# Self-attention scores from the 32 rows of each head, without the spread tile of keys

## The reference

```python
def _L1_attn_ref(x, W_qkv, b_qkv):            # H = 16 heads of D = 32
    b, t, _ = x.shape
    qkv = x @ W_qkv.T + b_qkv
    qkv = qkv.reshape(b, t, 3, H, D)
    q, k, v = (qkv[:, :, 0], qkv[:, :, 1], qkv[:, :, 2])
    q = _rope(q)
    k = _rope(k)
    q, k, v = (a.transpose(0, 2, 1, 3) for a in (q, k, v))
    scores = jnp.einsum('bhqd,bhkd->bhqk', q, k) / math.sqrt(D)
    w = jax.nn.softmax(scores, axis=-1)
    out = jnp.einsum('bhqk,bhkd->bhqd', w, v)
    return out.transpose(0, 2, 1, 3).reshape(b, t, E)
```

## Time and profile before

| | us |
|---|---|
| median of 3 runs | 2239.01 |
| the three runs | 2239.91, 2229.99, 2239.01 |
| the profiled execution | 2236.96 |
| its span (first to last instruction) | 2235.2 |
| projection block and its layer norm, from about 1972 to 2046.9 | 75 |
| attention block, from 2046.9 to 2085.1 | 38 |

### The profile page before, as it was taken

How to read it: one execution, slowest core, us unless ns; L and a number is a source line. 1 busy time by engine, 2 the same in 40 slices (tenths; PEclk the granted TensorE clock), 3 DMA queues, 4 the chain that set the end, 5 groups by cost and what they waited for, 6 DMA issues and landing times. The chain is left out here.

```text
span 2235.2 us, 44143 instructions
## 1 busy us (share of the span) xinstructions
PE 1971.9 (88%) x17800; PEld 1086.3 (49%) x17800; DVE 1626.0 (73%) x2842; ACT 994.2 (44%) x1404; POOL 680.1 (30%) x704
## 2 busy tenths in 40 slices
PE   6799999999597366999999999999999999767896
PEld 3355555555344223455555555555555555434542
DVE  4689999999565773587777777777777776446676
ACT  2689899989310332233333333333333333202332
POOL 3344444444210450133333333233333332121010
PEclk9899999999698577999999999999999999888898
DMA  4332333232131301000000000000000000110400
GB/s 142 96 80 73 87 95 89 69 82 58 31 136 52 127 1 58 21 22 19 4 22 22 21 22 22 21 22 22 21 22 22 21 2 2 48 71 0 156 0 19
DMA packets 40090, 106.16 MB, mean 47 GB/s; under 512 B 19280, under 2 KB 21584, under 8 KB 33744
## 3 DMA queue, kind: packets, MB, share of 16 engines
q1 hardware_dynamic: 39888, 103.35, 15.1%
HBM read 75.42 MB, written 1.05 MB: 34 GB/s over the span
## 5 line engine op out<-in xcount | busy, mean ns | idle before, releaser
L1360 POOL TENSOR_SCALAR a1c_p_hi<-a1c_pf 128x512 f16<-128x512 f32 x272 | 202.5, 745 | 663.8 <-ACT a1c_pf L1416 620.2
L365 POOL TENSOR_SCALAR a0c_p_hi<-a0c_r 128x1024 f16<-128x1024 f32 x128 | 154.9, 1210 | 268.9 <-DVE a0c_r L465 266.0
L1385 ACT ACTIVATE a1c_k_hi<-PS 128x512 f16<-128x512 f32 x136 | 81.2, 597 | 326.8 <-PE PS L1222 326.8
L470 DVE TENSOR_TENSOR a0c_p_lo<-a0c_r,a0c_p_hi 128x1024 f16<-128x1024 f32 x128 | 201.5, 1574 | 0.9 <-POOL a0c_p_hi L365 0.9
L1565 DVE TENSOR_TENSOR a1c_p_lo<-a1c_pf,a1c_p_hi 128x512 f16<-128x512 f32 x272 | 197.9, 729 | 5.5 <-POOL a1c_p_hi L1360 5.5
L1392 ACT ACTIVATE a1c_v_hi<-PS 128x512 f16<-128x512 f32 x136 | 81.6, 600 | 258.8 <-PE PS L1232 206.0
L1416 ACT ACTIVATE a1c_pf<-PS,a_maskc 128x512 f32<-128x512 f32 x256 | 175.1, 685 | 47.7 <-PE PS L1727 40.1
L1508 DVE CUSTOM_DVE_ANT_0 a1c_junk<-PS,a1c_maskr 128x512 bf16<-128x512 f32 x256 | 175.7, 686 | 18.4
L465 DVE TENSOR_TENSOR a0c_r<-PS,a0c_r 128x1024 f32<-128x1024 f32 x128 | 155.3, 1213 | 34.1 <-ACT a0c_r L411 34.0
L1483 DVE SCALAR_TENSOR_TENSOR a1c_k_lo<-PS,a1c_k_hi 128x512 f16<-128x512 f32 x136 | 93.8, 689 | 106.6 <-ACT a1c_k_hi L1385 106.6
L1490 DVE SCALAR_TENSOR_TENSOR a1c_v_lo<-PS,a1c_v_hi 128x512 f16<-128x512 f32 x136 | 93.9, 691 | 86.6 <-ACT a1c_v_hi L1392 85.1
(11 more groups left out here) (358 smaller groups left out, 4784.7 us busy)
## 6 DMA issues: line engine op xcount, KB each, us to landing
a_cf<-in_ctxT SPq DMA_DIRECT2D x16, 1024.0 KB, 5.1
a0c_ks<-a0c_k_hi SPq DMA_DIRECT2D x128, 128.0 KB, 2.3
a1c_cf<-in_ctx SPq DMA_DIRECT2D x16, 1024.0 KB, 4.8
a0c_ks<-a0c_k_lo SPq DMA_DIRECT2D x64, 128.0 KB, 2.4
f_w<-in_w SPq DMA_DIRECT2D x4, 1024.0 KB, 8.7
f_w<-in_w SPq DMA_DIRECT2D x1, 4096.0 KB, 19.6
s1q_w<-in_L1a_wT SPq DMA_DIRECT2D x3, 1024.0 KB, 7.7
w_gate_raw<-in_w_gate SPq DMA_DIRECT2D x1, 2816.0 KB, 10.4
```

The lines of the kernel that those rows point to most:

```text
L365: nc.gpsimd.tensor_scalar(p_hi[:, u % 4, :], r[:, u % 4, :], 1.0, 0.0, ALU.mult, ALU.add)\
L470: nc.vector.tensor_tensor(p_lo[:, u % 4, :], r[:, u % 4, :], p_hi[:, u % 4, :], ALU.subtract)\
L1360: nc.gpsimd.tensor_scalar(p_hi[:, v % 4, :], pf[:, v % 2, :], 1.0, 0.0, ALU.mult, ALU.add)\
```

## The change

The tile `kd` goes, and with it its clearing. In its place stands `kT`, laid out as `qT` is, filled by one copy of 128 rows for each bank. A unit is no longer the four heads of one f, but the four heads that lie in the same 32 rows j of the four f. Its scores are four matmuls with 32 rows each, 128 queries stationary and 128 keys moving, side by side in the unit's bank. The rest follows from this: which value tile each output uses, where it lands in its bank, and which columns of x a normalisation adds to (four pieces of 64 instead of one of 256).

```diff
-        qT, kd, v = m.sb("qT", [P, KT, D]), m.sb("kd", [P, B, KT, HG * P]), m.sb("v", [P, B, H, W])
+        qT, kT, v = m.sb("qT", [P, KT, D]), m.sb("kT", [P, KT, D]), m.sb("v", [P, B, H, W])
...
-                    nc.gpsimd.memset(kd[:], 0.0).then_inc(cleared, 1)
                     nc.gpsimd.memset(v[:, :, :, W - 1:W], 1.0).then_inc(cleared, 1)
...
-                    dve.wait_ge(cleared, 2)
+                    dve.wait_ge(cleared, 1)
...
                         dve.wait_ge(turned, KT + f + 1)
-                        for h in range(HG):
-                            r = slice(h * DH, (h + 1) * DH)
-                            nc.vector.tensor_copy(kd[r, :, f, h * P:(h + 1) * P],
-                                                  g.PS[r, KT + f, :].rearrange("p (b n) -> p b n", b=B))\
-                                .then_inc(k_out, 1)
+                        nc.vector.tensor_copy(kT[:, f, :], g.PS[:, KT + f, :]).then_inc(k_out, 1)
...
                     def score(n):
-                        b, f = n // KT, n % KT
+                        b, j = n // HG, n % HG
+                        rows, tokens = slice(j * DH, (j + 1) * DH), slice(b * P, (b + 1) * P)
                         if n >= 3:
                             pe.wait_ge(less_done, n - 2)
-                        nc.tensor.matmul(g.PS[:, n % 3, :], qT[:, f, b * P:(b + 1) * P], kd[:, b, f, :],
-                                         start=True, stop=True).then_inc(scores, 1)
+                        for f in range(KT):
+                            mm = nc.tensor.matmul(g.PS[:, n % 3, f * P:(f + 1) * P], qT[rows, f, tokens],
+                                                  kT[rows, f, tokens], start=True, stop=True)
+                        mm.then_inc(scores, 1)
...
                         pe.wait_ge(copied, n + 1)
-                        for h in range(HG):
-                            at = (4 * (f % 2) + h) * W
-                            mm = nc.tensor.matmul(g.PS[:, 5 + o % 3, at:at + W], pT[:, n % 4, h * P:(h + 1) * P],
-                                                  v[:, b, 4 * f + h, :], start=True, stop=True)
+                        for f in range(KT):
+                            at = (2 * f + j % 2) * W
+                            mm = nc.tensor.matmul(g.PS[:, 5 + o % 3, at:at + W], pT[:, n % 4, f * P:(f + 1) * P],
+                                                  v[:, b, 4 * f + j, :], start=True, stop=True)
...
-                        cols = slice(256 * half, 256 * half + 256)
+                        cols = slice(64 * half, 64 * half + 64)
+                        x = g.x[:, b, :].rearrange("p (f n) -> p f n", f=KT)[:, :, cols]
...
-                        nc.vector.tensor_tensor(g.x[:, b, cols], g.x[:, b, cols], y[:, b, cols], ALU.add)\
+                        nc.vector.tensor_tensor(x, x, y[:, o, :].rearrange("p (f n) -> p f n", f=KT), ALU.add)\
                             .then_inc(x_done, 1)
```

More of the change, by code:

```diff
@@ L1954, in self_attention_1 @@
             p, pT = s.sb("p", [P, 4, HG * P]), s.sb("pT", [P, 4, HG * P])
-            top, rec, y = s.sb("top", [P, N, HG]), s.sb("rec", [P, B, H]), s.sb("y", [P, B, D])
+            top, rec, y = s.sb("top", [P, N, HG]), s.sb("rec", [P, B, H]), s.sb("y", [P, 2 * B, D // 2])
             scores, top_done, less_done, exp_done = (s.sem(n) for n in ("scores", "top_done", "less_done", "exp_done"))
@@ L1978, in output @@
                     def output(n):
-                        b, f = n // KT, n % KT
-                        o = 2 * b + f // 2
-                        if o >= 3 and f % 2 == 0:
+                        b, j = n // HG, n % HG
+                        o = n // 2
+                        if o >= 3 and j % 2 == 0:
                             pe.wait_ge(y_done, o - 2)
                         pe.wait_ge(copied, n + 1)
-                        for h in range(HG):
-                            at = (4 * (f % 2) + h) * W
-                            mm = nc.tensor.matmul(g.PS[:, 5 + o % 3, at:at + W], pT[:, n % 4, h * P:(h + 1) * P],
-                                                  v[:, b, 4 * f + h, :], start=True, stop=True)
+                        for f in range(KT):
+                            at = (2 * f + j % 2) * W
+                            mm = nc.tensor.matmul(g.PS[:, 5 + o % 3, at:at + W], pT[:, n % 4, f * P:(f + 1) * P],
+                                                  v[:, b, 4 * f + j, :], start=True, stop=True)
                         mm.then_inc(outputs, 1)
@@ L2018, in normalise @@
                         dve.wait_ge(rec_done, o + 1)
-                        nc.vector.tensor_tensor(y[:, b, cols].rearrange("p (h n) -> p h n", h=8), out[:, :, 0:DH],
+                        nc.vector.tensor_tensor(y[:, o, :].rearrange("p (h n) -> p h n", h=8), out[:, :, 0:DH],
                                                 rec[:, b, hs].unsqueeze(2).to_broadcast([P, 8, DH]), ALU.mult)\
```

## The result

The changed kernel takes 2258.97 us (median of 4 runs, 2257.64 to 2261.97), the kernel before 2238.06 (4 runs). The ratio is 1.0102, with a 95% interval of 1.0079 to 1.0125: 1% slower, 21 us, where 2233.3 with a range from 2224 to 2242 was forecast. The profiled execution took 2261.97 us, its span is 2260.2. In this document a run that stands over 1.5% above the fastest of its kernel counts as slow and is left out of the ratios; that is one run, the longest of halves64.

The account below looks back on a forecast made before the run. DVE's key copies bound the first block and PE the loop; -8.6 (copies) - 1.0 (clock) + 0.8 + 3.1 (kind changes) = -5.7 us, giving 2233.3 us against the 2239.01 median, range 2224 to 2242.

Parts of the forecast that it names:

- Part 1: Block ahead of the loop: four 128-row key copies replace 16 on DVE, ending near 2038.0 instead of 2046.57; -8.6 us.
- Part 2: Clearing of the spread key tile on POOL, 6.92 us: nobody waits for it, so dropping it is worth 0.
- Part 3: Start of the attention loop: PE begins at full instead of half clock, so DVE starts earlier; -1.0 us.
- Parts 4 and 5: Loop's score matmuls, four for one (-0.04 us), plus two tile-kind changes (0.32): unit 2.19 to 2.47, +0.8 and +3.1 us.
- second rival: Score weight loads in the same 32 rows do not hide: 0.86 us per unit, +12.0, 2245.3 us; chance 0.08.
- third rival: Quarter-row score matmuls lose PE's 2.4 GHz clock in the loop: +14 us, 2253, up to 2270; chance 0.04.
- Part 5: Loop's changes between 32-row and 128-row tiles: 0.09 us each plus 0.07 for an open float32 load, two per unit, 0.32.

Follow-up runs that it names:

- halves64: Changed kernel with 64-row score matmuls, queries written twice with the other heads zeroed, nothing left out; median 2233.14 us over 12 runs, ratio 0.9988.
- bank_copies: Kernel before, with four 128-row key copies into an unread tile and the old loop on the cleared tile, keys left out; 2230.14 us.
- rows96: Changed kernel with scores taken over 96 rows (three heads summed, scores not the reference's), placed as 128-row matmuls; 2224.45 us, loop 37.4.
- rows64: Changed kernel with scores taken over 64 rows (two heads summed, scores not the reference's); 2225.62 us, loop 41.0, single execution.
- filler1024: Changed kernel with two unused 512-column float32 matmuls on all 128 rows ahead of each unit's four scores; 2256.04 us, loop 68.0.
- dense_first: Changed kernel with ten unused float32 matmuls of 512 columns on all rows ahead of the first score matmul; 2264.14 us, loop 70.3.
- keys_first: Kernel before, loop unchanged, keys transposed first and their copies split between ScalarE and VectorE; 2229.13 us, then 2227.13 in five rounds, ratio 0.9953.
- rows32_wide: Changed kernel with one 512-column score matmul on 32 rows per unit instead of four of 128 columns, scores not the reference's; 2259.36 us.
- split128: Kernel before, with each unit's score matmul cut into four of 128 columns on all 128 rows, each with its own weights; 2235.06 us.
- filler256: Changed kernel with one unused 256-column float32 matmul on all 128 rows ahead of each unit's four scores; 2275.27 us, loop 86.8.
- quads32: Changed kernel with four units' scores issued together, taking turns among four groups of 32 rows, each unit in its own bank; 2229.89 us, loop 45.4.

## Why the prediction was wrong

- *Part 1, the copies:* right. 8.6 us forecast, 15.15 - 6.70 = 8.45 measured, and the same 8.4 in bank_copies and rows96.
- *Part 2, the clearing:* right as far as the runs show. The stretch from the first projection matmul to the first transpose of q is 47.15 us with and without it.
- *Part 3, the clock at the start:* right in bank_copies, where the loop became 1.1 us shorter (1.0 forecast). In the changed kernel the first maximum came 1.16 us after PE's start, as forecast, and the clock fell about 1.1 us after that start, so that the gain was lost right after.
- *Parts 4 and 5, the matmuls and the changes of kind:* right in their sum at full clock. Unit of 2.49 us in rows64 for 2.47 forecast, 4.0 us between its loop and that of bank_copies for 3.9. With 32 rows the clock was full only at the start of some loops and in filler1024, but there the scores cost the same: 1.08 us from their start to the turns in dense_first, 1.09 in rows64. That the sum is so near is in part luck, since two small errors cancel: four matmuls in place of one cost +0.04 in rows96 (2.23 - 2.19) where -0.04 was forecast, and the two changes of kind 0.26 (2.49 - 2.23) where 0.32 was. The rule of the Trainium skill that stood behind the second rival (TensorE: Matmul & The Clock Gate, Part 3: a load overlaps a running matmul only when their row groups differ) did not hold: in the changed kernel, at half clock, a unit's eight score records, all in the same 32 rows, start (2.07 - 0.42) / 7 = 0.24 us apart, and the transposes of the same width and on all rows (1.11 - 0.42) / 3 = 0.23, so no load stood open between them.
- *The step that failed* is that the sum took the loop's clock as 1.00 and so had no term for it: +2.9 us for the loop (3.9 less 1.0), where +33.95 was measured, because the clock was 0.50 from 1.1 us after its start. The third rival, "the clock falls in the loop", had the mechanism and was given 0.04. What spoke against it was read wrongly twice. The clock of 1.00 in the earlier trace rows stood beside scores on 128 rows, and said nothing on 32. That the clock rose during transposes (full rows) was no evidence either. The rows of before could not have settled it: the 64-row matmuls of the earlier trace rows run in pairs, one in each half of the rows, so both halves are at work there, at a clock of 1.00; one 64-row matmul at a time, in halves64, lost the clock in the traced run.
- *Its size* was wrong as well: it had +1.2 us for each unit "at least" and 2253. The unit went from 2.49 at full clock (rows64) to 4.59, +2.10, since the outputs and the changes of kind doubled too; its far end, 2270, allowed for slower outputs. The measured 2259 lies between.
- The stage's sum as measured: -8.45 for the block, +33.95 for the loop, +0.7 behind it and -1.2 ahead of it give the spans' +25.0.

## What to carry to other kernels

Before cutting a contraction into row tiles, ask what keeps PE's clock up in that loop: a matmul that fills the other rows with zeros was the cheaper one here, because everything else on PE ran at its clock. A gain on the engine ahead of the loop is better sought there, as keys_first does, without touching the dense work. And a version near the edge, as halves64, has to be timed many times; a single execution, as of rows64, can show only its good side.

## What the runs showed of the hardware

- The granted clock in a loop with PE at work all the time went with the rows that its score matmuls used, one matmul at a time: 0.50 with 32 (rows32_wide, the changed kernel); 1.00 in rows64 and 1.00, then 0.50 in halves64 with 64; 1.00 with 96 (rows96) and 128 (split128). At full clock their units were within 2.19 to 2.49 us. Zeros in those rows did no harm: three quarters of `kd` are zero.
- More work made the loop faster: with full-row matmuls of 1.72 us added to each unit, all sixteen fillers counted, 69.9 us in place of 72.1 (filler1024). 0.43 us of them for each unit left the clock at 0.50 (filler256).
- A change between 128 rows and 64 costs 0.09 us in float16; in float32 0.13 (2.49 - 2.23, two of them), which by the prediction's Part 5 has a weight load in it that stands open; the runs do not part the two.
- The four groups of 32 rows ran at once: four units' scores took 2.09 us, one unit's 2.07 (quads32, the changed kernel, both at half clock).
- VectorE's copy from PSUM takes 0.69 us for 512 columns, be it 32 rows or 128 (the changed kernel).
